# Cross-attention and feed-forward chain on one core: pair weights loaded by SyncE, GpSimd's long operations in 256-column steps, the root's offset on GpSimd, scatters by block of 128 tokens, and a new written order on four engines

## The reference, cut to what matters

```
x = x + xattn0(layernorm(x), ctx)     # 16 heads of 16, q k v and output projection, with biases
x = x + ffn0(layernorm(x))            # h = relu(n w1 + b1); y = n + h w2 + b2; layernorm(y)*gamma + beta
x = x + xattn1(layernorm(x), ctx)     # layernorm again inside, one head of 256, scores * 256**-0.5
x = x + ffn1(layernorm(x))            # token at place s: n @ W[e(s)].T + b[e(s)], 8 experts
e(s) = argmax_t( pe(s) . sign(sig[t]) )   # by the token's place alone
```

## Time and profile before

| | |
|---|---|
| median of three runs | 297.12 us (297.0 to 298.82) |
| the profiled execution | 296.64 us, its span 294.8 us |
| busy: PE, DVE, ACT, POOL | 260.7, 212.1, 195.3, 139.1 us |
| mean granted clock of PE | 0.953 |
| first to last matmul | 6.05 to 284.5 us |

### The profile page before, as it was taken

The page is one execution under the profiler, slowest core; times in us unless marked ns, Lnnn a source line. Parts: engine busy times, 40 slices in busy tenths (PEclk is TensorE's granted clock), DMA queues, the critical chain, the costliest instruction groups (busy, mean ns, idle before and its releaser), DMA issues.

```text
span 294.8 us, 6416 instructions
## 1 busy us (share of the span) xinstructions
PE 260.7 (88%) x2080; PEld 230.1 (78%) x2080; DVE 212.1 (72%) x584; ACT 195.3 (66%) x798; POOL 139.1 (47%) x218
## 2 busy tenths in 40 slices
PE   1879778829999999999989999999999999999960
PEld 1659656528979899899879997879989999878740
DVE  2899797936968954854975386797598798988440
...
DMA packets 9085, 15.97 MB, mean 54 GB/s; under 512 B 1302, under 2 KB 6973, under 8 KB 8797
## 3 DMA queue, kind: packets, MB, share of 16 engines
q1 hardware_dynamic: 7133, 10.33, 10.4%
...
...
## 4 chain that ended last, share of the span: by engine, by line
PE 63%; DVE 13%; issue 7%; POOL 7%; ACT 7%; DMA 1%; POOLq 0%; SPq 0%; DVEq 0%; ACTq 0%
PE PB L234 29%; PE PB L227 12%; PE PB L371 5%; PE S L359 5%; POOL out_x L1251 5%; PE S L347 5%; PE PB L309 4%; ACT E L1030 3%; DVE SM L592 2%; DMA WKV<-in_w_k 1%; PE PB L274 1%; DVE X L724 1%; PE S L357 1%; DVE HL L658 1%; POOL X L1239 1%
## 5 line engine op out<-in xcount | busy, mean ns | idle before, releaser
L1030 ACT ACTIVATE E<-S,SX 128x77 f32<-128x77 f32 x256 | 79.0, 364 | 14.1 <-DVE SX L635 8.0
L1179 POOL TENSOR_TENSOR SM<-SM,nhalf 128x2 f32<-128x2 f32 x40 | 29.6, 741 | 85.6 <-DVE SM L598 84.8
L1030 ACT ACTIVATION_READ_ACCUMULATOR E<-S,SX 128x1 f32 x256 | 62.4, 246 | 0.0
L234 PE MATMUL PB<-XTH,W1H 128*128 128x256 f32 x128 | 37.7, 294 | 1.1 <-DVE XN L665 0.5
L234 PE MATMUL PB<-W2H,HH 128*128 128x256 f32 x128 | 37.7, 295 | 0.2 <-DVE HL L658 0.2
L234 PE MATMUL PB<-XTL,W1H 128*128 128x256 f32 x128 | 36.2, 282 | 0.0
L234 PE MATMUL PB<-XTH,W1L 128*128 128x256 f32 x128 | 36.1, 282 | 0.0
L234 PE MATMUL PB<-W2H,HL 128*128 128x256 f32 x128 | 35.7, 279 | 0.0
L234 PE MATMUL PB<-W2L,HH 128*128 128x256 f32 x128 | 35.7, 279 | 0.0
L635 DVE TENSOR_REDUCE SX<-S 128x8 f32<-128x616 f32 x32 | 24.6, 791 | 5.5 <-PE S L347 5.4
L442 PE MATMUL PB<-WD,XP 128*128 x120 | 28.2, 383 | 0.2
...
## 6 DMA issues: line engine op xcount, KB each, us to landing
...
X<-in_x SPq DMA_DIRECT2D x4, 256.0 KB, 6.3
x<-X SPq DMA_DIRECT2D x4, 256.0 KB, 2.1
...
RAW<-in_w_q SPq DMA_DIRECT2D x1, 256.0 KB, 4.2
Wo<-in_w_o SPq DMA_DIRECT2D x1, 256.0 KB, 6.3
```

Of the source, the lines that this page charges most:

```text
L234: t = e.matmul(dst, a, b, start=first and j == 0, stop=last and j == n - 1)
L1030: t = e.activation(E[:, i, a, h * NK:(h + 1) * NK], P[:, at:at + NK], ACT.Exp, bias=SX[:, i, 0, k:k + 1], accum_out=SX[:, i, 1, k:k + 1])
L1179: e.tensor_tensor(sm(K, g, 9), sm(K, g, 8), nhalf[:, :], ALU.pow).then_inc(s["rs" + K], 1)
```

## The change

**Weights by pair.** The input `WD` is laid out by expert (8 blocks of 128 rows by 512). SP, no longer PE, reads the 15 expert starts from `EV`, and loads each pair's weights (256 KB) by a DMA of its own, with its own semaphore, to a fixed place: pairs 0 to 7 in the room of `WD`, 8 to 11 in `E`, 12 and 13 in `RT` (both free after the first attention), 14 in a new tile. `starts()` on DVE and ACT stays, at new places.

```diff
+        def weights_of(n):
+            if n < 8:
+                return WD[:, n // 4, n % 4 * 512:(n % 4 + 1) * 512]
+            if n < 12:
+                return E[...][:, (n - 8) * 512:(n - 7) * 512]
+            return RT[:, n - 12, :, :]... if n < 14 else OWN[:, :]
 def pr(b, r, p):
-                w.wait_ge(s["wd"], 32)
+                    w.wait_ge(s[f"wd{n}"], 16)
-                                     WD[:, c, bass.ds(start[n], 256)], start=c == 0, stop=c == 1)
+                                     weights_of(n)[:, c * 256:(c + 1) * 256], start=c == 0, stop=c == 1)
 def sync(e):
+            def load_weights(which):
+                for n in which:
+                    load(f"wd{n}", weights_of(n), A["WD"][bass.ds(first[n], 128), :])
...
+            w.wait_ge(s["route2"], 1)
+            load_starts(e, 0, 7 * 128, first)
             w.wait_ge(s["ei"], 1)
             w.wait_ge(s["p_f"], 7)
-            for c in range(2):
-                load("wd", WD[:, c, :], A["WD"][c * 128:(c + 1) * 128, :])
+            load_weights(range(8))
+            load_weights((14,))
             for g in range(4):
                 w.wait_ge(s["x3"], g + 1)
                 load("kept", x3[...], X[:, g, :, :])
+            w.wait_ge(s["tE"], 32)
+            load_weights(range(8, 12))
+            w.wait_ge(s["wo"], 8)
+            load_weights((12, 13))
```

```diff
 def stats(K, g):
-                settle()
-                e.tensor_scalar(sm(K, g, 8), sm(K, g, 7), scale, add, ALU.mult, ALU.add).then_inc(s["var" + K], 1)
 def rs(K, g):
+                e.tensor_tensor(sm(K, g, 8), sm(K, g, 7), (epsC if K == "C" else eps1)[:, :],
+                                ALU.add).then_inc(s["ve"], 1)
+                w.wait_ge(s["ve"], 2 + eps_added[0])
                 e.tensor_tensor(sm(K, g, 9), sm(K, g, 8), nhalf[:, :], ALU.pow).then_inc(s["rs" + K], 1)
 def bo(g):     # and be, b2, bd in the same way; w_lo in steps of 256
-                e.tensor_tensor(X[:, g, :, :], X[:, g, :, :], rows(BO), ALU.add).then_inc(s["bo"], 1)
+                for i in range(2):
+                    t = e.tensor_tensor(X[:, g, i, :], X[:, g, i, :], bc[:, BO, :], ALU.add)
+                t.then_inc(s["bo"], 1)
-            def put(g):
-                w.wait_ge(s["pa"], 8 * (g // 4) + g % 4 + 5)
+            def put(b, m):
+                w.wait_ge(s["pa"], 8 * b + (m + 7) // 2 + 1)
```

**The order** of all four lists is new. The two places that the prediction follows, PE first, from `tA(3, ..)` and from the last `w2` on:

```diff
-  tA(3, 1); pv(0, 1); wo(0, 0); q(3, 1); tE(1, 0, 0, 0); tE(1, 0, 1, 1); tE(1, 1, 0, 0); tE(1, 1, 1, 1);
-  pv(1, 0, 0); sc(2, 0, 0, 0); sc(2, 0, 1, 1); pv(1, 1); starts(); tB(0, 0); wo(1, 3); sc(2, 1, 0, 0);
-  sc(2, 1, 1, 1); tA(4, 2); w1(0, 0, 0); w1(0, 1, 3); q(4, 2); ...
+  tA(3, 1); tE(1, 0, 0, 1); tE(1, 0, 1, 0); tB(0, 3); tE(1, 1, 0, 1); tE(1, 1, 1, 0); q(3, 1);
+  sc(2, 0, 0, 0); sc(2, 0, 1, 1); pv(1, 0, 0); pv(1, 1); w1(0, 0, 3); wo(1, 0); w1(0, 1, 3); w1(0, 2, 0);
+  sc(2, 1, 0, 0); w1(0, 3, 3); w2(0, 0, 0, 1); ...
...
-  w2(7, 1, 1); tC(6, 2); pr(0, 0, 1); cs(6, 2); tD(2, 3); pr(0, 1, 0); tD(3, 3); pr(0, 2, 1); cp(5, 3);
-  pr(0, 3, 0); co(5); tC(7, 2); tD(4, 1); cp(6, 0); cs(7, 2); co(6); pr(0, 4, 1); cp(7, 2); pr(0, 5, 0);
-  co(7); pr(0, 6, 1); tD(5, 2); pr(0, 7, 0); pr(1, 0, 3); tD(6, 0); pr(1, 1, 1); tD(7, 0); pr(1, 2, 3); ...
+  w2(7, 1, 1); tD(3, 0); tC(6, 2); pr(0, 2, 3); cs(6, 0); pr(0, 3, 2); pr(0, 4, 1); pr(0, 5, 3); tC(7, 0);
+  pr(0, 6, 2); cp(6, 3); cs(7, 0); co(6); tD(4, 0); pr(0, 7, 2); cp(7, 3); co(7); tD(5, 2); pr(1, 0, 0);
+  tD(6, 2); pr(1, 1, 3); tD(7, 2); pr(1, 2, 0); ...
```

DVE, ACT and POOL at the same places:

```diff
 DVE
-  ... x1(0); stats("B", 0); ssum(1, 1, 1); r_pairs(); smax(2, 0, 0); smax(2, 0, 1); apply("B", 0); o(1);
-  apply("A", 4); starts(); x1(1); lo("B", 0); ...
+  ... apply("B", 0); ssum(1, 1, 0); stats("A", 4); ssum(1, 1, 1); kbl(1); lo("A", 3); r_pairs();
+  smax(2, 0, 0); lo("B", 0); smax(2, 0, 1); o(1); f_norm(); hl(0, 0); x1(1); ...
+  f_kv(0); f_kv(1); ssum(3, 0, 0); starts(); smax(3, 1, 0); smax(3, 1, 1); lo("A", 4); ...
 ACT
-  ... apply("B", 0); et(1, 1, 1); starts(); ex(2, 0, 0); ex(2, 0, 1); hi("B", 0); apply("A", 4); ... hh(0, 0); ...
+  ... hi("A", 3); et(1, 0, 0); rr(1, 1, 1); et(1, 0, 1); hi("B", 0); et(1, 1, 0); et(1, 1, 1); qh(3);
+  starts(); hh(0, 0); ex(2, 0, 0); hh(0, 1); ex(2, 0, 1); ...
 POOL
-  ... bd(4); rs("D", 5); bd(5); put(0); rs("D", 6); put(1); rs("D", 7); put(2); bd(6); bd(7); put(3); ... put(7)
+  ... bd(4); rs("C", 7); put(0, 0); put(0, 1); put(0, 2); put(0, 3); put(0, 4); put(0, 5); rs("D", 6);
+  put(0, 6); rs("D", 7); bd(5); bd(6); bd(7); put(0, 7); put(1, 0); ... put(1, 7)
```

More of the change, by code:

```diff
@@ L59, in flat2, with apart, apart_upto @@
     return T.rearrange("p a b -> p (a b)")
+def apart(g, i, a):
+    return False
+def apart_upto(n):
+    return sum(apart(m // 4, m % 4 // 2, m % 2) for m in range(n + 1))
 def program(nc, A, out):
@@ L938, in vector @@
-            r_position(); ssum(1, 0, 0); vb(1); ql(2); r_index(); smax(1, 1, 0); ssum(1, 0, 1); apply("A", 3)
-            f_stats(); smax(1, 1, 1); o(0); ssum(1, 1, 0); lo("A", 3); stats("A", 4); x1(0); stats("B", 0)
-            ssum(1, 1, 1); r_pairs(); smax(2, 0, 0); smax(2, 0, 1); apply("B", 0); o(1); apply("A", 4); starts()
-            x1(1); lo("B", 0); ssum(2, 0, 0); ssum(2, 0, 1); smax(2, 1, 0); smax(2, 1, 1); lo("A", 4); stats("B", 1)
-            ql(3); ssum(2, 1, 0); hl(0, 0); hl(0, 1); f_norm(); ssum(2, 1, 1); apply("B", 1); hl(0, 2); ql(4)
@@ new lines, in vector @@
+            pivot(1); ssum(0, 0, 1); stats("A", 3); smax(0, 1, 0); smax(0, 1, 1); lo("A", 1); pivot(2); ssum(0, 1, 0)
+            r_expert(); ssum(0, 1, 1); apply("A", 2); ql(1); r_position(); smax(1, 0, 0); lo("A", 2); apply("A", 3)
+            smax(1, 0, 1); o(0); r_index(); smax(1, 1, 0); ssum(1, 0, 0); x1(0); ssum(1, 0, 1); stats("B", 0)
+            smax(1, 1, 1); ql(2); f_stats(); apply("B", 0); ssum(1, 1, 0); stats("A", 4); ssum(1, 1, 1); kbl(1)
+            lo("A", 3); r_pairs(); smax(2, 0, 0); lo("B", 0); smax(2, 0, 1); o(1); f_norm(); hl(0, 0); x1(1)
@@ new lines, in vector @@
+            stats("A", 5); stats("B", 1); hl(0, 1); ssum(2, 0, 0); ql(3); smax(2, 1, 0); ssum(2, 0, 1); apply("B", 1)
+            hl(0, 2); hl(0, 3); smax(2, 1, 1); apply("A", 4); stats("A", 6); lo("B", 1); vb(1); y(0); stats("Y", 0)
+            ssum(2, 1, 0); ssum(2, 1, 1); x2(0); stats("C", 0); hl(1, 0); hl(1, 1); hl(1, 2); smax(3, 0, 0)
+            smax(3, 0, 1); apply("C", 0); hl(1, 3); f_kv(0); f_kv(1); ssum(3, 0, 0); starts(); smax(3, 1, 0)
+            smax(3, 1, 1); lo("A", 4); apply("A", 5); stats("A", 7); y(1); stats("Y", 1); ql(4); ssum(3, 0, 1)
@@ new lines, in vector @@
+            ssum(3, 1, 0); f_m(); o(2); f_q(); ssum(3, 1, 1); x1(2); stats("B", 2); smax(4, 0, 0); f_c()
+            apply("B", 2); lo("A", 5); f_o(); apply("A", 6); x2(1); cm(0); stats("C", 1); lo("B", 2); o(3)
+            smax(4, 0, 1); smax(4, 1, 0); ssum(4, 0, 0); ql(5); x1(3); stats("B", 3); ssum(4, 0, 1); lo("A", 6)
+            apply("A", 7); apply("C", 1); apply("B", 3); hl(2, 0); hl(2, 1); ssum(4, 1, 0); lo("B", 3); hl(2, 2)
+            hl(2, 3); smax(4, 1, 1); smax(5, 0, 0); ssum(4, 1, 1); y(2); ssum(5, 0, 0); stats("Y", 2); hl(3, 0)
@@ L1210, in be @@
                 w.wait_ge(s["biB"], g + 1)
-                e.tensor_tensor(X[:, g, :, :], X[:, g, :, :], rows(BETA), ALU.add).then_inc(s["be"], 1)
+                for i in range(2):
+                    t = e.tensor_tensor(X[:, g, i, :], X[:, g, i, :], bc[:, BETA, :], ALU.add)
+                t.then_inc(s["be"], 1)
             def one(g):
@@ L1223, in b2 @@
                 w.wait_ge(s["xc"], g + 1)
-                e.tensor_tensor(Y, Y, rows(B2), ALU.add).then_inc(s["b2"], 1)
+                for i in range(2):
+                    t = e.tensor_tensor(Y[:, i, :], Y[:, i, :], bc[:, B2, :], ALU.add)
+                t.then_inc(s["b2"], 1)
             def sx(g):
@@ L1238, in bd @@
                 x = X[:, g, :, :]
[L1239 removed]
+                for i in range(2):
+                    t = e.tensor_tensor(x[:, i, :], x[:, i, :], BS[:, 2 * (g % 4) + i, :], ALU.add)
+                t.then_inc(s["bd"], 1)
             def bs(n):
@@ L1265, in sync @@
+            put(1, 2); put(1, 3); put(1, 4); put(1, 5); put(1, 6); put(1, 7)
         def sync(e):
```

263 lines of the change are left out of this document (138 added, 125 removed), and 1 row of the table SIGNALS.

## The result

The changed kernel took 301.95 us (median; 299.49 to 303.97) beside 297.97 us for the kernel before: a ratio of 1.011, with an interval of 1.006 to 1.017. The forecast was 286.8. The profiled execution took 299.49 us with a span of 297.6. In a later batch (one batch is a set of kernels run in turn on one chip beside their own runs of the kernel before) the same kernel took 288.95 us beside 295.65, a ratio of 0.981 [0.972, 0.990]. What parts the two is the main finding, so both profiles are read here. The ratios leave disturbed executions out, so they can differ a little from a quotient of the medians.

A forecast was written before the change was run, and what follows sets the result against it. PE's own work was taken to bound 70.6 to 247.4 us, with holes in the start-up, around 60 us and at the end. From 296.6 us, 6.0 for weights and registers and 3.8 for the tail gave 286.8, range 282 to 291.

The forecast's parts named there:

- is kept up to 247 us only because PE is the bound there, with nothing to run into: Middle of the kernel: PE's 6.0 us lead from around 60 us was to last until the last `w2`.
- POOL holds the tail: Rival, at the end: six scatters before `rs("D", 6)` and more small POOL work lose the tail's gain; 290.6 us, chance 0.08.
- Registers and lead: Around 60 us: without PE's register reads and with the new order, PE gets 6.0 us ahead, bounds 2 and 7.6.
- Staggered reads: Rival: ACT and DVE read registers at different times, each starving PE; 300.4 us, chance 0.11 together with late loads.
- Root offset and 256-column steps: DVE's 40 offset operations go to POOL, and POOL's long operations are split: both put at nothing outside the tail.
- one small step replaces another: 0 here: Root offset, on a normalisation's path: POOL's small addition replaces DVE's operation; 0, bounds -0.1 and +0.3 us each.
- DVE's gain from shorter blocks lies beside PE's work: 256-column steps: DVE's shorter waits on POOL were to save nothing in the kernel's time.
- The tail: After the last `w2`: 43.6 us against 47.4, counting the 5.0 us moved ahead, so -3.8 us, bounds 0 and -5.
- the 5.0 us of work moved ahead: Two `pr`, one `tD`, one `cp` and one `co` go ahead of the end of the last `w2`.
- After `rs("D", 7)` everything on POOL is back to back: Tail: three `bd`, `put(0, 7)` and eight scatters run without gaps to 35.0 us after the last `w2`, landed at 38.6.

The follow-up runs named there:

- w1: Kernel before with only each pair's weights fetched by SP's DMAs, so PE reads no registers, in the old order: ratio 1.000 with late signals, 1.002 without.
- e4: Changed kernel's code with the kernel before's order on all four engines, PE's register reads taken out: 292.49 us, 0.985, then 293.31 us, 0.993, both without late signals.
- e2: Changed kernel with POOL's rows of gathers bs and sx broken by other POOL work, scatters left: 0.973 and 0.983 without late signals, 0.992 with.
- e1: Kernel before with POOL's gathers bs and sx put in unbroken rows: 1.006 and 1.019 of the kernel before without late signals, 1.026 with.
- e6: Changed kernel with row bs broken, sx gathers cut into twos by spacers, scatters left in a row of six: 292.7 us, 0.987, with late signals.

## Why the prediction was wrong, and where it was right

**The failed step** is one clause: the lead "is kept up to 247 us only because PE is the bound there, with nothing to run into". There was something to run into: PE's late completion signals, beside two of POOL's unbroken rows of indirect DMAs. They cost 3.5 and 5.4 us of lead in the measured execution, and none where no signal was late. I had read POOL's list for its busy time and its dependences and never asked what a longer row of one kind of instruction does to the others. In the measured execution the last `w2` ends at 254.4 us, where 246.4 follow from 247.4 - 6.0 + 5.0, and in the tail, where signals are up to 2.5 us late beside the scatters, the gain of 1.1 us that the later batch shows turned into a loss of 0.8. The sum in its own terms is 296.6 + 2.0 (a lag, in place of the lead of 6.0) + 0.8 (the tail, in place of -3.8) = 299.4, against 299.49 measured. No rival named it; "POOL holds the tail" came nearest, and for another reason.

The trace of before did have a hint: up to the last scatters its rows are of one to four, and the signal of `pv(4, 1)` is 1.1 us late beside two gathers. I hadn't set increments beside the ends of matmuls.

**Registers and lead** ("6.0 us"): right in size, +7.1 and +5.3 us at 75 us in the two executions, and in the batch without late signals it stands at 6.6 by the last `w2`. In the measured execution `EV` was also written 1.6 us earlier than I took it (56.46 in place of 58.06 us), which the sum did not have. But the reason was only half of it. w1 takes the reads from PE in the old order. It starts the scores behind `wo(1)` at 64.32 us in place of 69.05, 4.7 us ahead, is 0.9 ahead at 75 us, and ends at 1.000: waits of 1.3 and 0.4 us take over, and the matmuls of `w1` between 68.8 and 72.0 us take 0.41 us in place of 0.28, at the lower clock. The lead comes from the new order, with `w1` and `wo(1)` ready while ACT reads; without the reads gone from PE, that order wasn't tried.

**Staggered reads** (rival, 300.4 us): did not happen. PE is busy for 15.00 of 15 us from 75 to 90 us in both executions. That the time came out near this rival's is chance.

**Root offset and 256-column steps** ("0 here", "nothing"): mis-sized. Alone they gave 0.991 and 0.989 of 298.3 us, or 2.6 and 3.2 us; together in the old orders 2.3 and 3.9 (e4's medians in two batches, all of it theirs, as w1 has none). The intervals are 2 to 6 us wide, so that the sum of two being more than both is no finding. For the offset, what failed is "one small step replaces another: 0 here"; what it gains by, the runs do not show. The new addition did not stand behind DVE, which would have made it slower: its 40 took 188 to 268 ns each. For the steps, it is "DVE's gain from shorter blocks lies beside PE's work". PE was busy for 174.4 of 176.8 us there, but a stretch that looks full has its small waits, and the tail has no cover at all. The row that would have told me was L694, at 540 ns for an operation that takes 170 when undisturbed, on the way from `tC` to `cp`. The page SBUF — State Buffer of the Trainium skill (Who interferes with whom) says that a `tensor_scalar` of VectorE can run in a mode that uses two ports, and that it and a GpSimd instruction then block each other for a whole instruction. The smaller stall beside halved instructions agrees with it; which mode these ran in no run here shows.

**The tail** ("-3.8 us"): mis-sized. Without late signals the time from the last `w2` to the end is 41.3 us, where 38.6 was forecast; with the 5.0 us of work moved ahead that is a gain of 1.1. My sum had the path of PE too short. I let PE stand for 0.2 us up to `tD(7)`; it stood for 1.4 (0.43 before `tC(7)`, 0.62 before `co(7)`, 0.34 before `tD(6)`), and its steps took about 1 us more than their prices. So `tD(7)` ends 22.3 us after the last `w2` where I had 20.1, and `pr(1, 3)` at 25.9 in place of 23.6. `put(0, 7)` is issued 1.5 us later than I had it, and the eight scatters behind it are not back to back from the start: two wait for DVE's sums, 1.25 and 0.77 us, and these sums wait for PE.

```profile
261.63 1.13 PE L248 MATMUL PB<-M,PTT 77*128 77x256 f32 x4 [0.62 <-ACT PTT L1102]
...
265.27 0.66 PE L330 MATMUL PB<-ident,XN 128*128 128x128 f32 x4 [0.34 <-DVE XN L624]
...
270.93 1.04 POOL L1296 DMA_INDIRECT out_x<-X,SI  x1 [0.16 <-issue]
271.82 1.11 DVE L747 SCALAR_TENSOR_TENSOR X<-PB,MK,X 128x256 f32 x2 [0.62 <-PE PB L457]
273.21 0.96 POOL L1296 DMA_INDIRECT out_x<-X,SI  x1 [1.25 <-DVE X L747]
273.55 1.11 DVE L747 SCALAR_TENSOR_TENSOR X<-PB,MK,X 128x256 f32 x2 [0.62 <-PE PB L457]
274.94 0.96 POOL L1296 DMA_INDIRECT out_x<-X,SI  x1 [0.77 <-DVE X L747]
```

From 274.94 us on they are back to back. DVE also waits for POOL's `bd` once, 1.61 us up to 268.22, but it waits for PE again at 270.10. So PE, not POOL, sets when the last scatters can start; "After `rs("D", 7)` everything on POOL is back to back" was wrong.

So where no signal is late the sum reads 296.6 - 6.6 - 1.1 = 288.9, against 288.93 for that profiled execution; the forecast of 286.8 is 2.1 us off it, 2.7 by the tail less 0.6 by the lead.

**What stays open.** Why some batches show late signals and others don't: neither the kernel nor the chip decides it, and within a batch the executions agree. What in the chip PE's signals and POOL's indirect DMAs share: I saw increments of PE held and let go in bursts, and ACT's, DVE's and POOL's beside them on time, no more. Why rows of the same length differ: a row of four made signals 3.1 to 3.6 us late in e2 and 0.8 us at 220.9 us in the kernel before, e1's `sx` row of eight 1.4, the last ten scatters none. The changed kernel with its scatters alone broken was not run in a batch with late signals, nor was the unaltered one in the same batch as e2 and e6; its 1.011 and 1.012 against their 0.992 and 0.987 are each against their own runs of before. Which of e6 and the unaltered kernel to take depends on the batch: 0.987 against 1.012 with late signals, e2's 0.983 against 0.981 without.
